# A new order of TensorE's work in the attention units of a transformer layer: transposes, scores, products, weighing

## The reference

```
xq, xk = rms_norm(x @ wq.T), rms_norm(x @ wk.T)      # 32 heads of q, 8 heads of k and v, width 64
xv = x @ wv.T
dist = pos[None, :] - pos[:, None]
allowed = (dist <= 0) & (dist >= -256)                # sliding window
bias = where(allowed, slope[h] * dist, -inf)
attn = softmax(einsum('bhtd,bhsd->bhts', xq, xk) / 8 + bias)
out = einsum('bhts,bhsd->bhtd', attn, xv)  ->  (b, t, 2048) @ wo.T
...
x = x + layernorm(attention(layernorm(x)))
x = x + layernorm(silu(g) * u @ down.T * down_s)      # g, u from layernorm(x), 1408 wide
```

## Time and profile before

| | |
|---|---|
| median of 3 runs | 1289.93 us (1289.88 to 1290.95) |
| the profiled execution | 1292.3 us |
| its span, first to last instruction | 1290.5 us |
| PE busy | 1202.0 us, 93% |
| DVE busy | 944.1 us, 73% |
| ACT busy | 758.4 us, 59% |
| mean granted TensorE clock | 0.989 of full |

### The profile page before, as it was taken

How to read it: one execution, slowest core, us unless ns; L and a number is a source line. 1 busy time by engine, 2 the same in 40 slices (tenths; PEclk the granted TensorE clock), 3 DMA queues, 4 the chain that set the end, 5 groups by cost and what they waited for, 6 DMA issues and landing times.

```text
span 1290.5 us, 29717 instructions
## 1 busy us (share of the span) xinstructions
PE 1202.0 (93%) x9016; PEld 1009.0 (78%) x9016; DVE 944.1 (73%) x2514; ACT 758.4 (59%) x2013; POOL 389.4 (30%) x459
## 2 busy tenths in 40 slices
PE   5999999997988999999999999999979979999998
PEld 4868778785766778889888898888867758888876
DVE  4597776857989898888888888888854346646364
ACT  3645454554888897877777777777732234232330
POOL 1000000002588775453535444443421100202021
PEclk9999999998999999999999999999989989999999
DMA  4216263455576555544546455554442252111120
GB/s 164 98 74 245 110 232 130 186 199 198 184 248 219 188 175 183 176 157 156 171 157 193 141 186 163 159 168 150 150 151 98 98 181 81 66 33 66 34 66 34
DMA packets 99262, 189.24 MB, mean 147 GB/s; under 512 B 8032, under 2 KB 36832, under 8 KB 99168
## 3 DMA queue, kind: packets, MB, share of 16 engines
q1 hardware_dynamic: 99168, 188.07, 42.7%
HBM read 116.48 MB, written 71.57 MB: 146 GB/s over the span
## 4 chain that ended last, share of the span: by engine, by line
PE 70%; DVE 12%; issue 8%; ACT 4%; POOL 3%; DMA 2%; DVEq 0%; ACTq 0%; POOLq 0%; SPq 0%
PE bank L1247 17%; PE bank L1378 17%; PE bank L1315 12%; PE bank L1278 8%; PE bank L1269 7%; DVE u_sb L1026 3%; ACT p_sb L825 2%; PE bank L1294 2%; PE bank L1304 2%; PE bank L1296 2%; PE bank L1295 2%; DVE pT_lo L1033 2%; DVE inv_rms L980 2%; POOL bias L607 1%; POOL qk L642 1%
## 5 line engine op out<-in xcount | busy, mean ns | idle before, releaser
L825 ACT ACTIVATE p_sb<-u_sb,low 128x384 f32<-128x384 f32 (+2 forms) x512 | 273.7, 535 | 74.5 <-DVE low L1026 47.5
L1026 DVE CUSTOM_DVE_ANT_0 u_sb<-bank,bias 128x384 f32<-128x384 f32 (+2 forms) x512 | 231.7, 453 | 37.2 <-PE bank L1269 17.8
L1033 DVE TENSOR_TENSOR pT_lo<-bank,pT_hi 128x384 f16<-128x384 f32 (+2 forms) x512 | 232.4, 454 | 28.9 <-ACT pT_hi L833 18.7
L1269 PE MATMUL bank<-k_st,q_st 128*128 128x384 f32 (+2 forms) x1024 | 247.2, 323 | 4.4 <-DVE v_out L1000 2.9
L1278 PE MATMUL bank<-ident,p_sb 128*128 128x128 f32 x1152 | 220.9, 282 | 29.1 <-DVE pT_lo L1033 19.2
L833 ACT ACTIVATE pT_hi<-bank 128x384 f16<-128x384 f32 (+2 forms) x512 | 204.0, 398 | 45.4 <-PE bank L1278 43.6
L1269 PEld LDWEIGHTS bank<-k_st,q_st 128*128 128x128 f32 x1024 | 175.4, 191 | 27.7 <-DVE v_out L1000 3.3
L1278 PEld LDWEIGHTS bank<-ident,p_sb 128*128 128x128 f32 x1152 | 137.1, 141 | 75.9 <-ACT p_sb L825 49.9
L580 POOL TENSOR_TENSOR rstd<-var_eps,minus_half 128x1 f32<-128x1 f32 (+1 forms) x31 | 23.3, 752 | 492.1 <-DVE var_eps L921 492.1
L617 POOL TENSOR_TENSOR o_mid<-o_raw,inv_sum 128x256 f32<-128x256 f32 x128 | 84.1, 657 | 241.1 <-DVE o_raw L1047 239.5
L1294 PE MATMUL bank<-v_st,pT_hi 128*128 128x64 f16 x1152 | 154.7, 193 | 0.5 <-DVE pT_lo L1033 0.5
(11 more groups left out here) (115 smaller groups left out, 2424.1 us busy)
## 6 DMA issues: line engine op xcount, KB each, us to landing
q_scr<-qk SPq DMA_DIRECT2D x64, 512.0 KB, 2.7
q_st<-q_scr SPq DMA_DIRECT2D x32, 1024.0 KB, 7.8
k_st<-k_scr SPq DMA_DIRECT2D x64, 256.0 KB, 3.0
o_scr<-o_out SPq DMA_DIRECT2D x128, 128.0 KB, 2.6
o_in<-o_scr SPq DMA_DIRECT2D x16, 1024.0 KB, 5.3
k_scr<-qk SPq DMA_DIRECT2D x16, 512.0 KB, 2.8
z_in<-z_scr SPq DMA_DIRECT2D x8, 1024.0 KB, 6.0
x_in<-x SPq DMA_DIRECT2D x4, 1024.0 KB, 8.3
```

What stands on the lines that cost most here:

```text
L825: nc.scalar.activation(p_sb[:, u % RING, 0:w], u_sb[:, u % RING, 0:w], ACT.Exp, scale=-1.0, bias=low[:, u % RING:u % RING + 1], accum_out= ...
L1026: nc.vector.tensor_tensor_reduce(out=u_sb[:, u % RING, 0:w], in0=bank[u % 2][:, 0:w], in1=bias[:, 2 * u // UNITS, u % REP, at:at + w], sca ...
L1033: nc.vector.tensor_tensor(pT_lo[:, u % RING, 0:w], bank[2 + u % 2][:, 0:w], pT_hi[:, u % RING, 0:w], ALU.subtract).then_inc(pT_ready, 1)
L1269: mm = nc.tensor.matmul(bank[u % 2][:, 0:w], q_st[:, s, r, P * i:P * i + P], k_st[:, s, part, P * key:P * key + w], start=(part == 0), sto ...
```

## The change

The entries of `LAGS` are put in a new order, and transposes (with their rounding) move from two slots back to three. PE's slot now goes T of unit u-3, To, S of unit u, P, W of unit u-4. ACT's goes R of unit u-3, E of unit u. DVE's goes B of unit u, Sp of unit u-3, then the rest. No instruction is added or removed, no DMA is moved.

```
-LAGS = {"split": 3, "scores": 0, "transpose": 2, "exps": 0, "invert_sums": 1, "weigh": 4, "take": 5}
+LAGS = {"transpose": 3, "scores": 0, "split": 3, "exps": 0, "invert_sums": 1, "weigh": 4, "take": 5}
...
-            def unit_work(n, u):
+            def unit_work(n, u, kinds=("transpose", "scores", "weigh")):
                 for stage, nn, uu in due(n, u):
                     work = {"scores": scores, "transpose": transpose_p, "weigh": weigh_values}.get(stage)
-                    if work:
+                    if stage in kinds:
                         work(nn, uu)
 
             def attend(n, tile=None):
                 for u in range(UNITS):
-                    unit_work(n, u)
+                    unit_work(n, u, ("transpose",))
                     if tile is not None:
                         m, at = divmod(u - START, STEP)
                         if m in range(4) and at == 0:
                             transpose_o(tile, m)
+                    unit_work(n, u, ("scores",))
+                    if tile is not None:
                         m, at = divmod(u - START - 4, STEP)
                         if m in range(4):
...
                             project_o(tile, m, (2 * at, 2 * at + 1), bank[7])
+                    unit_work(n, u, ("weigh",))
```

## The result

The changed kernel takes 1336.31 us (median of 4, 1335.49 to 1337.85) against 1290.44 for the kernel before on the same chip: a ratio of 1.0354, interval 1.0338 to 1.0369. The prediction had the direction; the time lies 27 us beyond its upper bound. The profiled execution took 1336.96, its span 1335.2 where it was 1290.5.

What follows compares the result with a forecast made beforehand. PE was taken to bound product slots, a DVE-ACT loop the full-width slots without products. Loop +8.8, group starts +7.2, weight loads -8.8 and end of attention +1 gave +8.2 on 1289.9: 1298 us, range 1283 to 1309.

Steps and rivals of the forecast that it cites:

- loop Sp, W, T, S, B, Sp: Full-width slots without products: a new loop through PE takes 1.27 us a slot against the present 1.12.
- a PEclk under 1 after group 0: Granted PE clock in groups after group 0: a value below 1 would show the forecast wrong.
- in the narrower slots ... I take +0.2 a group: Narrower slots of groups without products: both loops nearly equal, +0.2 us a group, between 0 and 2.4.
- in groups 1 and 2 ... I take 0.6 each: Groups 1 and 2: DVE's idle time takes up part of the loop's cost, +0.6 us each, between 0 and 2.6.
- group 0's 2.4: Group 0: extra work lies in narrow slots, so it loses only the full-width part, 2.4 us.
- in product slots the loop is harmless: Product slots: they last about 1.48 us, and P does not stand between W and the next S.
- start-of-group term: First slots of each group with products: about 0.65 us later, 11 groups, +7.2 us, bounds 0 and 13.
- weight loads -8.8: Product slots without a To: 0.04 us less exposed weight load each, -8.8 us in all, bounds 0 and -17.6.
- The clock rival: Lower PE clock in full-width slots of groups 0 to 4: +58 us beside the 8.2, 1356; chance 0.03.
- The faster one: Waits at T vanish and group starts give back 8.8 us: -7.8 us, 1282; chance 0.15.
- The one with no change: Weight loads give 17.6 us, or the new loop stays under 1.12 us: 1289; chance 0.12.
- slower rival with no saving: No saving in weight loads and a pile at the group's start: +17 us, 1307; chance 0.13.

Runs made afterwards that it cites:

- e3: Changed kernel with the weighing five units back instead of four and the take six instead of five; 1315.14 us, ratio 1.0184.
- e13: Changed kernel with the take of values six units behind the scores instead of five, nothing else; 1328.33 us, ratio 1.0283.
- e9: Changed kernel with the third leftover norm of groups 0 to 2 in DVE's slot 5 instead of 6; 1330.82 us, ratio 1.0318.
- e6: Changed kernel with the leftover norms of groups 0 to 2 cut to 16 of 512 columns; 1321.13 us, one run.
- e5: Kernel before with the leftover norms of groups 0 to 2 cut to 16 of 512 columns; 1281.23 us, one run.
- e4: Changed kernel with one added, unused PE matmul per slot in groups 0 to 4, to hold the clock up; 1336.74 us, ratio 1.0353.
- e11: Kernel before with the third leftover norm in DVE's slot 5 and the low half of oT one slot later; 1296.49 us, ratio 1.0050.
- e8: Kernel before with PE's new order (T, S, P, W) in every slot, lags and DVE's order unchanged; 1340.61 us, ratio 1.0390.

## Why the prediction was wrong in size

**Right.** The direction and its cause. The loop Sp, W, T, S, B, Sp exists, with the predicted members, at 1.23 us for 1.27; W waits and T does not. e3, which lets W wait a slot longer, gives 21 us back; the take that moves with it is worth 8 by itself (e13), which leaves 13 to the weighing if the two simply add. By stretch the prediction was off by 18.2 us in groups 0 to 2, by 2.5 in groups 3 and 4 and by 19.0 in groups 5 to 15, so two steps carry the miss: what the loop does to groups with side work, and what it does to product slots. One of its own signs of being wrong came, a PEclk under 1 after group 0 (0.84 and 0.88).

**The step "in the narrower slots ... I take +0.2 a group".** Group 4 measured +3.9, 2.6 predicted, but the split is the reverse of the prediction. The 16 full-width slots cost +1.05 where 2.4 was predicted: a run of eight starts with room to spare and reaches 1.23 a slot only in its second half (9.48 for eight, against 8.86). Slots 0 to 3 and 16 to 19 cost +1.2 each: their scores are narrow, but W and T in them still belong to full-width units. The prediction worked that very case out for the start of a group with products, 1.07 a slot against 0.88, and did not apply it to groups 0 to 4.

**The step "in groups 1 and 2 ... I take 0.6 each", and group 0's 2.4.** Measured 8.5, 6.1 and 7.2. The prediction let idle time of DVE absorb the loop, because DVE had other work. Nothing was absorbed: groups 3 and 4, without norms, lose 3.8 and 3.9 us to the loop, and with what e9 gives back (2.4 in group 1, 3.1 in group 2) that makes 6.2 and 6.9, beside 6.1 and 7.2 measured. This is a sum of two runs' numbers and not one experiment, but it leaves little over. The term for which the prediction had nothing is the second: in the new order the norm starts behind POOL's bias, stands still for 2 us and passes that on. In group 0 the bare loop is 2.9 (e6 against e5), e9 gives back 2.4 and the filler of e4 2.9. These add to 8.2 of 8.5, but e9 also raised the clock, from 0.73 to 0.80, so the last two overlap in part, and how the 5.6 us beside the loop split between held norms and clock stays open.

**The step "in product slots the loop is harmless".** True of a plain product slot, false of two slots in each group. The slack was read from slots without a take and an oT_lo. Where both stand ahead of B, slots 12 and 24 grew by 0.37 and 0.36 us. Slots 0 to 3 cost 0.70 (0.5 predicted) and the exit from the pile nothing (0.15 predicted). Slots 13 to 23 gave back 0.2. The sum is 1.2 us a group, 13 over eleven groups, and three falls of the clock, at 1.5 us, make up the rest of the 17.4. The start-of-group term was right; the term that was missing is that of slots 12 and 24, and e13 shows 0.3 us in each of them to be the pair's.

**The term "weight loads -8.8".** 0.02 a slot instead of 0.04, between 4 and 5 us in all (the product slots without a To are 21 a group, not 20). The row on To could not show that S, too, pays for a place behind T. The Trainium skill (TensorE: Matmul & The Clock Gate, LDWEIGHTS), whose rule the prediction set aside, would have given no saving. The 0.02 measured lies halfway between that and the prediction's row.

**The clock rival, at 0.03.** It was priced as a fall in every slot and dismissed since PE's waits are short. It came, in part: groups 0 to 2 were granted 0.73 to 0.88, at 3 us in group 0 (e4) and an unknown sum in groups 1 and 2, and of the groups with products 7, 11 and 15 had a fall, at 1.5 us each. One such fall of the changed kernel, in group 7: PE waited 0.66, 0.28 and 0.59 us for pT_lo in a row of three slots, and then the two matmuls of S took 0.98 us, where they take 0.60:

```profile
606.80 0.20 PE L1294 MATMUL bank<-v_st,pT_hi 128*128 128x64 f16 x1 [0.66 <-DVE pT_lo L1033]
...
609.14 0.20 PE L1294 MATMUL bank<-v_st,pT_hi 128*128 128x64 f16 x1 [0.59 <-DVE pT_lo L1033]
...
609.41 0.98 PE L1269 MATMUL bank<-k_st,q_st 128*128 128x384 f32 x2
```

The prediction held that waits as short as these leave the clock alone; here they did not. But they are not enough to foretell a fall: all eleven groups with products have three such waits at this place (in group 8: 0.67, 0.29 and 0.59), and eight of them kept the full clock. At least 7 us of the 45 are thus the clock's, on top of waits that have another cause.

**The other rivals.** The faster one is refuted: the waits at T vanished (0.0 on the page), and the new ones at W are larger. The one with no change needed 17.6 us of weight loads or a loop under 1.12: neither came. The one that lay nearest was the slower rival with no saving, and it missed for the same reasons as the forecast.

No version tried beats the kernel before. The nearest are its own variant with a later take (1293) and e11 (1296).

## What to carry to other kernels

When an order is changed on several engines, list the loops that close across them and how many slots each spans, for every kind of slot (narrow scores beside wide transposes, slots with an extra take or low half), not for the plain one. Where a loop has become the bound, do not count on side work to absorb it: groups 1 and 2 paid for the loop in full, and for a side operation that had moved beside an instruction of POOL. Try each engine's part alone: here DVE's order alone cost 61 us, PE's alone 50 (e8), and both with T a unit later 46. T a unit later, alone, was not run.

## What the runs showed of the hardware

A DVE operation that reads two SBUF tensors stood still while POOL ran one of its own: 16 columns took 2.79 us beside a bias of 2.75, and 0.23 otherwise. A norm that started 0.36 us ahead of the bias (kernel before) or 0.61 ahead (e13) went first, and the bias took 3.2 us instead of 2.75; one that started 0.01 ahead (e6) or 0.54 behind (changed kernel) was held until the bias ended. Waits of PE of 0.66, 0.28 and 0.59 us, with work between them, were followed by a stretch at the lower clock, 1.2 of 2.4 GHz, in three of the eleven groups that have three such waits, at 1.5 us each. What a place in PE's order costs depends on what stands in front of it: from its start to that of its successor P took 0.54 us behind W and 0.47 behind S, S 0.35 behind P and 0.43 behind T. Over a whole slot these changes came to 0.02.
